# A decoder layer on one core: PSUM banks given out by kind of product instead of from one queue of eight

## The reference

```python
x = x + L0_attn(layernorm(x))             # causal, 16 heads of 32, rotary on q and k
x = x + L0_xattn(layernorm(x), ctx_2048)  # see below
x = x + L0_ffn(layernorm(x))              # ternary weights, silu(gate) * up, RMS norm, projection
```

```python
ln_out = _ln(hidden_states, ln_w, ln_b)
q, k, v = ...            # fp8-rounded inputs times wq, wk, wv; q and k normalised per head of 128
core = _gqa(q, k, v)     # 16 query heads, 8 key heads, over the sequence itself
qx = ...                 # the same with wqx
kx, vx = jnp.split(jnp.einsum('bsi,oi->bso', cond, w_kv_x), 2, axis=-1)   # kx normalised
xout = _gqa(qx, kx, vx)  # over the context
catq = _div_clamp_fp8(jnp.concatenate([core, xout], axis=-1), proj_smooth)
return jnp.einsum('bsi,oi->bso', catq, wproj) * (proj_in_scale * proj_w_scale)
```

## Time and profile before

| | before |
|---|---|
| median of 3 runs | 1260.66 us (1259.59 to 1261.97) |
| profiled execution | 1259.75 us, span 1257.9 us |
| TensorE busy | 1195.8 us, 95% |
| VectorE busy | 938.0 us, 75% |
| ScalarE busy | 805.3 us, 64% |
| GpSimd busy | 607.8 us, 48% |
| granted TensorE clock, mean | 0.977 |

### The profile page before, as it was taken

One profiled execution on the slowest core, in us unless ns is written; L12 is line 12 of the kernel. 1 busy time (PEld: TensorE's weight loads), 2 busy tenths in 40 slices (PEclk: granted clock), 3 DMA queues, 4 the chain that ended last, 5 costly groups with the idle time before them and its releaser, 6 DMA issues.

```text
span 1257.9 us, 19385 instructions
## 1 busy us (share of the span) xinstructions
PE 1195.8 (95%) x6408; PEld 819.4 (65%) x6432; DVE 938.0 (75%) x2794; ACT 805.3 (64%) x2301; POOL 607.8 (48%) x722
## 2 busy tenths in 40 slices
PE   4999989889999999999999999999999997999998
PEld 2677767566676666667666677766767765565545
DVE  4679987999888887899999866667777877463341
ACT  4676557777877776577666675667777767652230
POOL 2538875643544545465455632224544443363470
PEclk9999988899999999999999999999999999899999
DMA  8230000011211121212323211041101100000000
GB/s 264 86 99 18 2 1 1 1 51 51 67 35 34 59 80 47 92 44 91 104 88 109 82 47 38 17 142 59 50 27 59 59 18 1 1 1 16 15 1 30
DMA packets 25460, 65.60 MB, mean 52 GB/s; under 512 B 2720, under 2 KB 8992, under 8 KB 25360
## 3 DMA queue, kind: packets, MB, share of 16 engines
q1 hardware_dynamic: 25088, 64.00, 16.2%
q10 hardware_dynamic: 272, 0.36, 0.1%
HBM read 59.37 MB, written 4.98 MB: 51 GB/s over the span
## 4 chain that ended last, share of the span: by engine, by line
PE 47%; DVE 27%; ACT 19%; POOL 4%; issue 2%; DMA 1%; ACTq 0%; POOLq 0%; SPq 0%
PE ps L855 9%; PE ps L1052 8%; PE ps L1119 8%; ACT big L785 6%; PE ps L845 4%; PE ps L1168 4%; PE ps L1014 3%; PE ps L947 3%; DVE big L412 3%; DVE big L967 3%; ACT big L950 2%; PE ps L979 2%; DVE big L240 2%; DVE big L655 2%; DVE big L656 2%
## 5 line engine op out<-in xcount | busy, mean ns | idle before, releaser
L855 PE MATMUL ps<-big 128*125 128x512 bf16 x1152 | 264.5, 379 | 0.5 <-ACT big L942 0.5
L785 ACT ACTIVATE big<-ps,big 112x128 f32<-112x128 f32 (+1 forms) x512 | 192.4, 456 | 72.6 <-POOL big L430 70.1
L855 PEld LDWEIGHTS ps<-big 128*125 128x125 bf16 x1152 | 155.2, 136 | 80.3 <-ACT big L942 0.8
L429 POOL TENSOR_TENSOR big<-big 112x4 f32<-112x4 f32 (+1 forms) x128 | 38.6, 302 | 319.7 <-ACT big L424 319.7
L845 PE MATMUL ps<-big 128*112 128x512 bf16 x768 | 187.4, 387 | 1.9 <-ACT big L942 1.0
L659 POOL TENSOR_TENSOR big<-big 128x448 f32<-128x448 bf16 x96 | 102.8, 1071 | 111.1 <-DVE big L964 70.1
L845 PEld LDWEIGHTS ps<-big 128*112 128x112 bf16 x768 | 99.8, 132 | 65.8 <-issue 6.4
L967 DVE TENSOR_SCALAR big<-big 112x112 f32<-112x112 f32 (+1 forms) x256 | 131.5, 534 | 6.8
L412 DVE BATCH_NORM_STATS2 big<-ps 112x6 f32<-112x128 f32 (+1 forms) x512 | 113.3, 283 | 20.1 <-PE ps L855 18.8
L1014 PE MATMUL ps<-big 125*128 125x224 f32 (+1 forms) x512 | 122.1, 362 | 5.5 <-DVE big L996 4.8
L950 ACT ACTIVATE big<-ps,big 112x375 f32<-112x375 f32 x128 | 74.6, 583 | 82.3 <-DVE big L949 81.2
(11 more groups left out here) (115 smaller groups left out, 2312.4 us busy)
## 6 DMA issues: line engine op xcount, KB each, us to landing
big<-in_ctx_t SPq DMA_DIRECT2D x32, 375.0 KB, 3.7
big<-in_w_s SPq DMA_DIRECT2D x16, 512.0 KB, 3.6
big<-in_w_p SPq DMA_DIRECT2D x16, 512.0 KB, 3.7
big<-in_w_x SPq DMA_DIRECT2D x16, 512.0 KB, 3.8
big<-in_w_g SPq DMA_DIRECT2D x16, 512.0 KB, 3.7
big<-in_w_d SPq DMA_DIRECT2D x8, 512.0 KB, 4.6
big<-in_w_a SPq DMA_DIRECT2D x8, 384.0 KB, 4.6
scr<-big SPq DMA_DIRECT2D x24, 128.0 KB, 1.7
```

What stands on the lines that cost most here:

```text
L785: t = act(lambda e, j=j: e.activation(z[0:rows, 128 * j:128 * j + 128], bk[0:rows, 128 * j:128 * j + 128], ACT.Identity, bias=rr[0:rows, 4 ...
L855: t = pe(lambda e, k=k, s=s, u=u, n=n: e.matmul(bk[0:CK, :], cT[:, s, k, CK * c:CK * c + CK], w[:, u, k, col:col + 512], start=n == 0, sto ...
```

## The change

The one pool becomes six. Each holds fixed banks, and each kind of product takes from its own and gives back to it:

| pool | banks | who takes |
|---|---|---|
| `bM` | 0, 1 | projections: `a_mm`, `p_mm` |
| `bX` | 2, 3 | transposes and sums: `a_tr`, `a_tq`, `l_2`, `lnb_t`, `f_1`, `b_m`, `t_s6` |
| `bS` | 4 | scores: `a_s0`, `t_s0` |
| `bP` | 5 | transposed P: `a_s2`, `t_s2` |
| `bO` | 6, 7 | products with v: `a_s3`, `t_s3` |
| `bG` | none at first | the last block: `g_0`, `d_0` |

`give` hands banks to `bG` as the second attention ends: three at tick `g_start`, one at `g_start + 4`, one at `g_start + 7`, two at `g_start + 12`; one stays in `bX`.

```diff
-        bank = Pool([(p[:, :], p[:, :].bitcast(BF)) for p in psum])
+        banks = [(p[:, :], p[:, :].bitcast(BF)) for p in psum]
+
+        def home(*which):
+            p = Pool(banks)
+            p.idle = [(i, []) for i in which]
+            return p
+
+        def give(src, dst, n):
+            for _ in range(n):
+                dst.idle.append(src.idle.pop(0))
+
+
+        bM, bX, bS, bP, bO, bG = home(0, 1), home(2, 3), home(4), home(5), home(6, 7), home()
...
         def p_mm(it):
...
-            bi, (bk, _), free = bank.take()
+            bi, (bk, _), free = bM.take()
...
         def lnb_z(it):
...
-            bank.release(it["bi"], t)
+            bM.release(it["bi"], t)
...
         def t_s0(it):
...
-            bi, (bk, _), free = bank.take()
+            bi, (bk, _), free = bS.take()
...
-            bank.release(bi, te)
+            bS.release(bi, te)
...
             if tick == g_start:
                 free_at[0] = all_now()
+                give(bM, bG, 2)
+                give(bX, bG, 1)
+            if tick == g_start + 4:
+                give(bS, bG, 1)
+            if tick == g_start + 7:
+                give(bP, bG, 1)
+            if tick == g_start + 12:
+                give(bO, bG, 2)
```

More of the change, by code:

```diff
@@ L351, in b_m @@
                 return
-            bi, (bk, _), bf = bank.take()
+            bi, (bk, _), bf = bX.take()
             tm = pe(lambda e: e.matmul(bk, oneb, u["a"].bitcast(BF), start=True, stop=True),
@@ L356, in b_m @@
             u["tc"] = act(lambda e: e.activation(sc, bk, ACT.Copy), tm)
-            bank.release(bi, u["tc"])
+            bX.release(bi, u["tc"])
         def b_2(u):
@@ L479, in a_tr @@
             h1 = it["h1"]
-            bi, (bk, _), free = bank.take()
+            bi, (bk, _), free = bX.take()
             for k in range(4):
@@ L492, in a_tl @@
             tl = dve(lambda e: e.tensor_tensor(xT[:, 1, :, :], b4, xT[:, 0, :, :], ALU.subtract), th)
-            bank.release(bi, tl)
+            bX.release(bi, tl)
             it["txT"] = [th, tl]
@@ L501, in a_mm @@
                 if n == 0:
-                    it[f"b{j}"] = bank.take()
+                    it[f"b{j}"] = bM.take()
                 bi, (bk, _), free = it[f"b{j}"]
@@ L553, in a_te @@
             te = act(lambda e: e.activation(qT, src, ACT.Copy), t, of)
-            bank.release(bi, te)
+            bX.release(bi, te)
             it[f"qT{j}"] = (oi, qT, te)
@@ L589, in a_s2 @@
             p = g["p"]
-            bi, (bk, _), free = bank.take()
+            bi, (bk, _), free = bP.take()
             for h in range(4):
@@ L604, in a_s2e @@
                 te = dve(lambda e: e.tensor_copy(pT[0:T], src), t, pf)
-            bank.release(bi, te)
+            bP.release(bi, te)
             g.update(pT=pT, pTi=i, tpT=te)
@@ L611, in a_s3 @@
             if c == 0:
-                it["ob"] = bank.take()
+                it["ob"] = bO.take()
             bi, (bk, _), free = it["ob"]
@@ L637, in a_s4 @@
                 ri.unsqueeze(2).broadcast_to([T, 16, 32]), ALU.mult), t, it["tpv"], zf, after)
-            bank.release(bi, t2)
+            bO.release(bi, t2)
             a_sm.release(i, t2)
@@ L690, in l_2 @@
                     bias=vc[:, V_LNB + k:V_LNB + k + 1], scale=vc[:, V_LNW + k:V_LNW + k + 1]), t, ff, t_c2)
-            bank.release(bi, tf)
+            bX.release(bi, tf)
             it["f"] = (fi, f, tf)
@@ L975, in t_s2 @@
             hl = it["hl"]
-            bi, (bb, _), free = bank.take()
+            bi, (bb, _), free = bP.take()
             rows, nn = (T, 2) if S else (CK, 3)
@@ L1008, in t_s3 @@
             if g % 2 == 0:
-                bt["ob"] = bank.take()
+                bt["ob"] = bO.take()
             bi, (bk, _), free = bt["ob"]
@@ L1038, in t_s4 @@
                            [it["tpv"], t_rsm], cfree)
-            bank.release(bi, t1)
+            bO.release(bi, t1)
             bt["tcat"].append(t5)
@@ L1059, in t_s6 @@
                 x1[0:T, b, :], bk[0:T, :], pscale[0:T, :], x1[0:T, b, :], ALU.mult, ALU.add), t, t_ps, x1tok[b])
-            bank.release(bi, t2)
+            bX.release(bi, t2)
             x1tok[b] = t2
@@ L1114, in g_0 @@
             for which in range(2):
-                bi, (bk, _), free = bank.take()
+                bi, (bk, _), free = bG.take()
                 n = 0
@@ L1128, in g_0 @@
             ts = act(lambda e: e.activation(h, bk[:, 0:448], ACT.Silu), t, hfree, after)
-            bank.release(bi, ts)
+            bG.release(bi, ts)
             it.update(h=h, hi=i, ts=ts)
@@ L1171, in d_0 @@
                     n += 1
-            ri, (rk, _), rfree = bank.take()
+            ri, (rk, _), rfree = bG.take()
             tr = pe(lambda e: e.matmul(rk[0:T, 0:1], acc[j][:, sl], cf[:, C_UNIT:C_UNIT + 1], start=True, stop=True),
@@ L1186, in d_1 @@
                 it["t"], it["t2"], x1tok[b])
-            bank.release(it["bi"], t)
+            bG.release(it["bi"], t)
             small2.release(it["si"], t)
```

12 lines of the change are left out of this document (5 added, 7 removed).

## The result

The changed kernel takes 1362.56 us (1361.04 to 1364.32), the kernel before 1261.32 in the runs beside it: ratio 1.0805, 95% interval 1.0786 to 1.0823, so 101.2 us slower. The direction and the range hold. The likeliest time, 1336, was 27 us too low, and the measured time lies above 1360, the upper end of that case's own range. Of the loss itself 75.4 us were forecast, 26 too few.

The account below looks back on a forecast made before the run. No engine alone was taken as the bound: most stages loop through TensorE and ScalarE or VectorE, though TensorE has no room in S and X1. Terms 6 + 8 + 18.7 + 22.7 + 11 + 9 = 75.4 gave 1336 us, range 1305 to 1395.

Parts of the forecast that it names:

- S: 270 to 455 us: two-bank projections wait for z, the last readers of a projection's bank; 24.5 less 5.8 idle, 18.7 us.
- X0: 455 to 757 us: scores wait for their single bank, then projections for z, 3.5 us per regular batch; 22.7 us (15 to 39).
- X1: 757 to 1055 us: one projection in each of eight batches waits 1.37 us for z; 11 us (8 to 22).
- the other priced reading: X1, 757 to 1055 us: the next projection's wait adds too, giving the upper bound of 22 us.
- Transition: 162 to 270 us: the wait for z moves ahead of a projection and two small groups, three places; 8 us (0 to 15).
- Attention: Causal attention, 30 to 162 us: scores wait for the exponential, mostly covered, 1 us per batch of six; 6 us.
- Last block: Gate products, 1055 to 1125 us: wait for banks that a SiLU frees, plus 2 us for transposes of f_1; 9 us (4 to 14).
- The clock as a rival: Every second of 24 stalls in S and X0 brings a half-clock stretch: 37 us on top, 1373 us; 20%.
- Hidden: Whole kernel: TensorE runs so far ahead that new waits are covered and only old ones go; 1250 us, 6%.
- partly hidden: Whole kernel: half of the summed loss is paid; about 1290 us, 7%.
- adding: Whole kernel: every new wait is paid in full, since readers move with TensorE; 145 us, 1405 us, 9%.

Follow-up runs that it names:

- fill: The changed kernel with six more products, read by nobody, ahead of each projection of k in S: 1354.22 us.
- late8: The kernel before, one queue of eight banks, but the bank of a normalised projection (z) is passed over by the next seven takes: 1259.53 us, ratio 0.9992.
- proj2: Against the changed kernel: only projections have banks of their own (two), all else shares one queue of six until the last block: 1329.57 us.
- proj3: Against the changed kernel: only projections have banks of their own, three, and all else shares one queue of five: 1278.66 us.
- both scores kernels: Against the changed kernel: only scores have banks of their own, one (rest share seven) or two (rest share six): 1299.9 and 1279.51 us.
- late8_fill: The kernel before with late banks for z, plus 34 unread products meant for five idle places of the transition: 1262.02 us.

## Why the prediction was right and wrong

- **S, 18.7 forecast, 25.1 measured.** The wait was right in its place and near in size: 16.3 us with the clock held (`fill`). Each wait was read as 2.05 to 2.53 and measured 1.56. The prediction gave back all 5.8 us of old idle time; `late8` shows that removing the old wait for z wins nothing alone, but here the old waits are gone from the list, since the new wait stands ahead of them, and 2.8 us for the scores' bank came instead. The rest, 8.3, is the clock.
- **X0, 22.7 against 24.8.** A regular batch cost 3.56 where 3.5 was chosen between 2.7 and 4.9. The mechanism was wider than told: projections, scores and transposed P all wait. That the number came so close is in part luck of the choice.
- **X1, 11 against 11.5.** 1.16 to 1.54 per batch against 1.37; the other priced reading, that every projection's wait adds, is out.
- **Transition, 8 against 10.7.** Within its bounds of 0 to 15. The clock is 0.89 in both kernels between the two marks, TensorE's busy time grows by 1.3 and its idle time by 9.4. Of the kernels with one kind apart only `proj2` loses much there (15.0, in an execution 8 us above its median), so the two banks of the projections are the likely cause, as forecast.
- **Attention, 6 against 16.5: the term furthest off**, though its upper bound was 25. By the two rows of the attention above, idle time grows by 5.6 (24.82 - 19.24), near the forecast, and busy time by 10.9, with the clock at 0.87 in place of 0.94. One place, 101.09, stood for all six sequences. It lies in the fourth sequence, and that one was read nearly right; the third was not. The third and the fourth, from first scores to first scores, before:

```profile
78.31:98.62 20.31, 19.57 (x137) 14.68 (x136) 15.35 (x27) 14.70 (x54) 8.99 (x8) 1.00 0.35 105
...
98.62:120.11 21.49, 20.86 (x137) 15.26 (x136) 20.84 (x37) 13.45 (x55) 18.14 (x17) 0.92 0.00 1
```

  and after:

```profile
85.42:111.59 26.17, 23.93 (x138) 17.84 (x136) 17.12 (x30) 16.35 (x58) 11.46 (x10) 0.80 0.27 81
...
111.59:133.55 21.96, 20.95 (x138) 15.86 (x136) 18.48 (x33) 12.56 (x52) 17.98 (x16) 0.92 0.00 1
```

  The fourth loses 0.5 us, with the clock at 0.92 in both kernels; the third loses 5.9, with the clock at 0.80 in place of 1.00. In the changed kernel five waits of the scores, each in a sequence's second group, total 7.5 us, for instance

```profile
90.47 0.62 PE L578 MATMUL ps<-big 112*112 112x448 bf16 x1 [2.02 <-ACT big L590]
91.02 1.83 PE L581 MATMUL ps<-big 32*112 32x112 f32 x8
```

  and each is followed by a stretch at half clock; in three of the five the scores take 1.83 in place of 1.03.
- **Last block, 9 against 12.7.** `proj2`, `proj3` and both scores kernels, which share its banks, lose 0.2 to 1.9 there, so the split is the cause. Between the two marks TensorE's idle time grows by 8.3, near the forecast, and its busy time by 4.4, with the clock at 0.95 in place of 0.97. TensorE's waits from 1139 to 1250 us name both parts of the forecast, L1131 (the gate products) and L1092 (the transposes of f_1); before, L1080 waited 7.7 in all:

```profile
PE ps L1092 <- DVE big L1102: 6.1, 2, 3.5
PE ps L1131 <- ACT big L1140: 3.4, 3, 2.3
...
PE ps L1131 <- DVE big L1149: 3.0, 3, 2.5
PE ps L1092 <- ACT big L1083: 2.8, 2, 1.5
```

- **The clock as a rival, not a term.** This is the step that failed: the sum put the clock at nothing, and gave it 20% and 37 us as a case of its own, in S and X0. Extra work that holds the clock in S and in the attention gives back 8.3 + 9.2 = 17.5 us, of which some 4 are lost before too. So some 13 of the 26 us that were missing are shown to be clock; the rest was not tested. The rival's mechanism is shown in S, at 8.3 us; in X0, after 26 waits, the changed kernel had one stretch at half clock; the attention, which the rival did not name, had more. Nor is every idle time followed by half clock, as the prediction put it: in S five of eleven were, in X1 none of eight. Forecast and rival were not alternatives: waits that stop TensorE can bring part of the clock's price with them.
- **Hidden, partly hidden, adding** are out: S pays the wait in full, and 35.3 would have been X0's sum without cover.

## What to carry to other kernels

A pool of buffers decides which earlier read an instruction waits for. Count, for each kind, how many of its own turns ago that read began: two projections ago cost 25 us in S, three ago 2.4, one queue of eight nothing. Where a new wait stops a TensorE that sets the pace, expect the clock on top of its price, and test it by giving the engine work that nobody reads. Look in the trace whether that work stands in the idle time: in `fill` it did, in `late8_fill` it came behind, and that run settled nothing.

## What the runs showed of the hardware

- Six products more per batch of S made the changed kernel 8.3 us faster (1362.56 to 1354.22): the granted clock of the eleven batches rose from 0.96 to 1.00.
- In the changed kernel, idle times of 0.9 to 2.2 us ahead of the attention's scores were each followed by half clock, those of 1.56 in S in five of eleven cases, and those of 0.7 to 1.4 in X1 never. What decides between them was not settled; in the kernel before the fourth sequence ran at 0.92 although its scores did not wait.
- The name behind an idle time can be wrong: L976 at 994.69 stood for z.
